# Self attention of a decoder layer: softmax sums as a ninth value column, division between two block transposes on DVE

## What is computed

```
# x: [8, 256, 128]; 16 heads of 8 features; all in float32
q, k, v = heads(x @ wq.T), heads(x @ wk.T), heads(x @ wv.T)     # [8, 16, 256, 8]
scores = einsum('bhtc,bhkc->bhtk', q, k) * 8 ** -0.5
scores = where(tril, scores, -inf)
attn = softmax(scores, axis=-1)                                 # exp(s - max) / sum of exp(s - max)
out = einsum('bhtk,bhkc->bhtc', attn, v)
x = layernorm(x + out.reshape(8, 256, 128) @ wo.T)
...                                                             # cross attention, then the experts
```

## Time and profile before

| what | us |
|---|---|
| median of 3 executions | 1145.12 (1144.67 to 1145.13) |
| the profiled execution, its own time | 1145.18 |
| its span, first to last instruction | 1143.1 |
| busy: PE, DVE, ACT, POOL | 1099.8, 879.7, 734.4, 539.8 |
| granted TensorE clock, mean | 0.998 of full speed |
| one batch of self attention (end to end) | 21.2 in the middle, 22.6 and 23.7 in the last full ones |
| self attention's last matmuls (line 692) | end at 193.9 |

### The profile page before, as it was taken

One profiled execution on the slowest core, in us unless ns is written; L12 is line 12 of the kernel. 1 busy time (PEld: TensorE's weight loads), 2 busy tenths in 40 slices (PEclk: granted clock), 3 DMA queues, 4 the chain that ended last, 5 costly groups with the idle time before them and its releaser, 6 DMA issues.

```text
span 1143.1 us, 27502 instructions
## 1 busy us (share of the span) xinstructions
PE 1099.8 (96%) x8781; PEld 945.9 (83%) x8781; DVE 879.7 (77%) x2778; ACT 734.4 (64%) x1754; POOL 539.8 (47%) x892
## 2 busy tenths in 40 slices
PE   6999988999999999999999999999999999999997
PEld 5888876788887887887888888888788887999997
DVE  7999998887787877777877878877878686655554
ACT  6999997766666766766765766666667565322221
POOL 4666774544564365446455445544644432400101
PEclk9999999999999999999999999999999999999999
DMA  2000011000000000000000000000000003000000
GB/s 93 7 7 11 7 44 37 3 11 1 1 1 11 2 1 11 1 1 11 2 1 1 11 2 1 2 1 2 1 2 1 2 1 97 2 10 6 7 10 11
DMA packets 14683, 12.38 MB, mean 11 GB/s; under 512 B 1360, under 2 KB 13648, under 8 KB 14416
## 3 DMA queue, kind: packets, MB, share of 16 engines
q1 hardware_dynamic: 14128, 10.43, 3.0%
q10 hardware_dynamic: 416, 0.20, 0.1%
HBM read 9.57 MB, written 1.05 MB: 9 GB/s over the span
## 4 chain that ended last, share of the span: by engine, by line
PE 65%; POOL 7%; issue 3%; ACT 1%; DVE 1%; POOLq 0%; DVEq 0%; ACTq 0%
PE ps L1163 12%; PE ps L1152 12%; PE ps L1146 11%; PE ps L1487 5%; POOL xk_parts L890 3%; PE ps L1478 3%; PE ps L1479 3%; PE ps L1480 3%; PE ps L1178 3%; PE ps L1136 2%; PE ps L1137 2%; PE ps L1138 2%; PE ps L1171 2%; PE ps L1118 2%; PE ps L1120 1%
## 5 line engine op out<-in xcount | busy, mean ns | idle before, releaser
L890 POOL TENSOR_TENSOR xk_parts<-k_raw,xk_parts 64x768 fp32r<-64x768 f32 x128 | 236.1, 1844 | 313.2 <-DVE xk_parts L1009 310.5
L1033 DVE CUSTOM_DVE_ANT_0 xmasked<-ps,bar 128x768 f32<-128x768 f32 x256 | 244.3, 954 | 4.3 <-issue 0.6
L946 ACT ACTIVATE xprobs<-xmasked,xlow 128x768 f32<-128x768 f32 x256 | 238.2, 930 | 1.3 <-DVE xlow L1033 1.0
L1146 PE MATMUL ps<-xk_parts,xq_parts 128*128 128x512 f32 (+1 forms) x1024 | 232.7, 349 | 2.7 <-ACT k_raw L926 1.3
L1152 PE MATMUL ps<-ident,xprobs 128*128 128x128 f32 x1536 | 215.2, 276 | 5.6 <-DVE xlow L1033 5.3
L1146 PEld LDWEIGHTS ps<-xk_parts,xq_parts 128*128 128x128 f32 x1024 | 173.7, 189 | 28.9 <-ACT k_raw L926 3.0
L1152 PEld LDWEIGHTS ps<-ident,xprobs 128*128 128x128 f32 x1536 | 168.8, 140 | 15.2 <-DVE xlow L1033 10.1
L1163 PE MATMUL ps<-xprobs_t,xvals 128*64 128x256 f32 x1536 | 179.9, 383 | 1.1 <-issue 1.1
L1163 PEld LDWEIGHTS ps<-xprobs_t,xvals 128*64 128x64 f32 x1536 | 104.8, 137 | 57.9 <-issue 11.9
L1038 DVE COPY xprobs_t<-ps 128x768 f32<-128x768 f32 x128 | 121.6, 950 | 2.0 <-PE ps L1152 2.0
L926 ACT ACTIVATE k_raw<-ps 128x768 f32<-128x768 f32 x64 | 52.0, 812 | 102.5 <-PE ps L1120 89.6
(11 more groups left out here) (220 smaller groups left out, 2526.9 us busy)
## 6 DMA issues: line engine op xcount, KB each, us to landing
ctx_in<-in_ctx SPq DMA_DIRECT2D x8, 256.0 KB, 3.2
w_rest<-in_L_ffn_w SPq DMA_DIRECT2D x2, 768.0 KB, 5.8
raw_kv<-in_L_xattn_Wkv SPq DMA_DIRECT2D x1, 1024.0 KB, 5.2
out<-state SPq DMA_DIRECT2D x8, 128.0 KB, 2.0
x_in<-in_x SPq DMA_DIRECT2D x7, 128.0 KB, 2.1
raw_q<-in_L_xattn_Wq SPq DMA_DIRECT2D x1, 512.0 KB, 6.0
wout<-in_L_xattn_Wout SPq DMA_DIRECT2D x1, 512.0 KB, 3.9
keep_all<-in_mask_BxS_bk SPq DMA_DIRECT2D x1, 512.0 KB, 5.2
```

The lines of the kernel that those rows point to most:

```text
L890: pool.tensor_tensor(k_parts[dst, i // 2 % 2, h, :], k_raw[src, :], k_parts[src, i // 2 % 2, h, :].bitcast(F32), ALU.subtract).then_inc(k_ ...
L946: nc.scalar.activation(probs[:, i % 4, :], masked[:, i % 4, :], ACT.Exp, scale=-1.0, bias=low[:, i % 4:i % 4 + 1], accum_out=sums[:, pair ...
L1033: dve.tensor_tensor_reduce(masked[:, i % 4, :], slot(slots.place("S", b, i), KEYS), bar[:, par, :], 1.0, 3e38, ALU.add, ALU.min, low[:, i ...
L1146: last = nc.tensor.matmul(slot(s, hi - lo, lo), q_parts[:, pair % 2, h, part, t * P:(t + 1) * P], k_parts[:, pair % 2, h, lo:hi], start=pa ...
```

## The change

The value blocks get a ninth column of ones, so that the PV matmuls give the sums of the exponentials beside the 8 features (row 32j+8 of the result for head j). The accumulator output of EXP is gone, and with it `sums`, `WIDE`, `R` and `rsum_t`. Per group DVE now does four steps: `TURN` transposes 32x32 blocks of the PV result, so that a token's features of a head stand side by side with their sum; `RECIP` takes the reciprocals of the sums; `DIVIDE` multiplies the 8 features by them; `NORM` transposes the blocks back into `heads_t`. PE's next PV into the same bank waits for TURN. Of the copies PT, ACT takes three of four heads and DVE the last of each group. The input is loaded into `state` directly, and OUT adds in place, so the loads don't wait for earlier batches. Setup gains two memsets on DVE. OUT moves to 24.5 in both tables, and a few cross attention steps on DVE (BAR, HI, TWICE) and the turn of its slots are shifted.

```diff
@@ DVE's steps of the cross attention that stand in the last units
-                               B: steps(emit, "Q", 1, 5, 1) + steps(emit, "BAR", 1, 7.6, 1) + steps(emit, "HI", 2, 5.8, 0.7)
-                               + steps(emit, "TWICE", 2, 6.2, 1.35)})
+                               B: steps(emit, "Q", 1, 5, 1) + steps(emit, "BAR", 1, 8.7, 1) + steps(emit, "HI", 2, 5.8, 1.4)
+                               + steps(emit, "TWICE", 2, 7.1, 1.5)})
...
-    x_in = sb(mem, "x_in", [P, 2, T, D])
...
-    sums = sb(mem, "sums", [P, 2, T, HG])
-    rsum = sb(mem, "rsum", [P, 2, T, HG])
-    rsum_wide = sb(mem, "rsum_wide", [P, 2, T, HG, 32])
-    rsum_t = sb(mem, "rsum_t", [P, 2, S])
+    turned = sb(mem, "turned", [P, 2, S // 32, 32])
+    rsum = sb(mem, "rsum", [P, 2, S // 32, 1])
+    divided = sb(mem, "divided", [P, 2, S // 32, 32])
...
+    def by_dve(h):
+
+        return h % HG == HG - 1
...
     pe_order = Order(B, SH, {
         "S": (SH, -0.5), "PT": (SH, 4.75), "K": (SG, -3.5), "Q": (SG, -4), "V": (1, 2),
-        "T": (1, -5), "R": (SG, 9.75), "PV": (SG, 9.5), "OUT": (1, 24),
+        "T": (1, -5), "PV": (SG, 9.5), "OUT": (1, 24.5),
...
     dve_order = Order(B, SH, {
-        "S": (SH, -0.5), "K": (SG, -3.5), "Q": (SG, -4.25), "PT": (SH // 2, 5.5),
-        "XLO": (1, -5.25), "RECIP": (SG, 5.75), "NORM": (SG, 10), "OUT": (1, 23.5),
+        "S": (SH, -0.5), "K": (SG, -3.5), "Q": (SG, -4.25), "PT": (SH, 4.5),
+        "XLO": (1, -5.25), "TURN": (SG, 10), "RECIP": (SG, 10.3), "DIVIDE": (SG, 10.6), "NORM": (SG, 11), "OUT": (1, 24.5),
...
-        "EXP": (SH, 3), "PT": (SH // 2, 6.75), "K": (SG, -1.75), "Q": (SG, -3), "R": (SG, 11.25),
+        "EXP": (SH, 3), "PT": (SH, 6.75), "K": (SG, -1.75), "Q": (SG, -3),
...
     pool_order = Order(B, SH, {
-        "Q_HEAD": (SH, 1.25), "WIDE": (SG, 10.75), "SPLIT": (3, 5.5, 5)})
+        "Q_HEAD": (SH, 1.25), "SPLIT": (3, 5.5, 5)})
...
@@ SP
-            wait(sp, added, b - 1)
             wait(sp, loaded_x, 16 * b)
-            sp.dma_start(x_in[:, par, :, :], x_rows[b]).then_inc(loaded_x, 16)
+            sp.dma_start(state[:, b * T:(b + 1) * T, :], x_rows[b]).then_inc(loaded_x, 16)
...
@@ ACT
-                if i % HG == 0:
-                    wait(act, rsum_ready, b * SG + g - 1)
...
                     nc.scalar.activation(probs[:, i % 4, lo:hi], masked[:, r, lo:hi], ACT.Exp,
-                                         scale=-1.0, bias=low[:, r, j:j + 1],
-                                         accum_out=sums[:, g % 2, j, i % HG:i % HG + 1]).then_inc(exp_done, 1)
+                                         scale=-1.0, bias=low[:, r, j:j + 1]).then_inc(exp_done, 1)
...
@@ DVE
-        dve.memset(vals[:, :, :, :, :], 0.0)
+        dve.memset(divided[:, :, :, :], 0.0)
+        link(dve.memset(vals[:, :, :, :, :], 0.0))
+        dve.memset(vals[:, :, :, :, SD:SD + 1], 1.0)
...
+            if kind == "TURN":
+                n = b * SG + i
+                dve.wait_ge(pv_done, n + 1)
+                wait(dve, divided_ready, n - 1)
+                dve.transpose(turned[:, i % 2, :, :].rearrange("p n c -> p (n c)"),
+                              ps[:, O_BANK + i % 2, 0:S]).then_inc(turned_ready, 1)
             if kind == "RECIP":
                 n = b * SG + i
-                dve.wait_ge(exp_done, T * HG * (n + 1))
-                wait(dve, wide_ready, n - 1)
-                dve.reciprocal(rsum[:, i % 2, :, :], sums[:, i % 2, :, :]).then_inc(rsum_ready, 1)
+                dve.wait_ge(turned_ready, n + 1)
+                dve.reciprocal(rsum[:, i % 2, :, :], turned[:, i % 2, :, SD:SD + 1]).then_inc(rsum_ready, 1)
+            if kind == "DIVIDE":
+                n = b * SG + i
+                dve.wait_ge(rsum_ready, n + 1)
+                wait(dve, heads_ready, n - 1)
+                dve.tensor_tensor(divided[:, i % 2, :, 0:SD], turned[:, i % 2, :, 0:SD],
+                                  rsum[:, i % 2, :, :].broadcast_to([P, S // 32, SD]), ALU.mult).then_inc(divided_ready, 1)
             if kind == "NORM":
                 n = b * SG + i
-                dve.wait_ge(rsum_t_ready, n + 1)
-                dve.wait_ge(pv_done, n + 1)
+                dve.wait_ge(divided_ready, n + 1)
...
-                dve.tensor_tensor(heads_t[:, i, :], ps[:, O_BANK + i % 2, 0:S], rsum_t[:, i % 2, :],
-                                  ALU.mult).then_inc(heads_ready, 1)
+                dve.transpose(heads_t[:, i, :], divided[:, i % 2, :, :].rearrange("p n c -> p (n c)")).then_inc(heads_ready, 1)
...
@@ PE, PV
-                pe.wait_ge(pt_act, (n + 1) * HG // 2)
-                pe.wait_ge(pt_dve, (n + 1) * HG // 2)
+                pe.wait_ge(pt_act, (n + 1) * (HG - 1))
+                pe.wait_ge(pt_dve, n + 1)
                 pe.wait_ge(v_ready, b + 1)
-                wait(pe, heads_ready, n - 1)
+                wait(pe, turned_ready, n - 1)
...
-    slots = Turns(pe_order, full, SLOTS, 2)
+    slots = Turns(pe_order, full, SLOTS, 1)
```

56 lines of the change are left out of this document (20 added, 36 removed).

## The result

The changed kernel is slower: 1148.53 us, median of 8 executions (1148.06 to 1148.94), against 1145.12 of the kernel before on the same chip; the ratio is 1.0029, with a 95% interval of 1.0020 to 1.0038. The prediction said 1142.3. The profiled execution has a span of 1146.5 us against 1143.1, so 3.4 us are to be found in the trace.

What follows compares the result with a forecast made beforehand. ACT was taken to bound the kernel, with DVE the bound afterwards. Against 1145.18 us, -4.0 for the batches, -0.4 for the late ones and +1.5 at the stage's end gave 1142.3 us; 8 in 10 range 1135 to 1152.

Steps and rivals of the forecast that it cites:

- What bounds the kernel before: Middle of the stage: ACT is the bound, busy 20.84 of 21.20 us a batch, with DVE busy 19.47.
- ACT after the change: ACT's work a batch falls from 20.7 to 18.2 us, with 0.70 a head instead of 0.88.
- DVE after the change: DVE's work a batch rises by 0.92 to 19.8 us, 1.14 added against 0.91 removed per group; DVE becomes the bound.
- The half rate case: Rival: DVE's 4-byte block transpose runs at half a copy's rate, giving a batch of 22.7 and 1158.7 us; chance 0.08.
- The meeting with POOL: DIVIDE on DVE is blocked while POOL masks heads, costing 0.4 us a batch; bounds 0 and 2.4.
- The rival in which every group meets a mask: DIVIDE meets a POOL head mask nearly each time, giving a batch of 21.7 to 21.8 and 1151.6 us; chance 0.18.
- Waits that stay: DVE's remaining stands at OUT, TURN and XLO cost 0.3 us a batch; bounds 0 and 1.0.
- Another limit close to 21 holds the pace: Rival: PE's matmuls or the PE, ACT and DVE loop around Q and K; 1144 to 1146.7 us; chance 0.26.
- The late batches: The two batches mixed with cross attention steps each take 0.2 us less, 0.4 together; bounds 1 us either way.
- The end of the stage: The last DIVIDE stalls beside POOL's 1.80 us instruction, delaying NORM and PE's OUT: 1.5 us more; bounds -0.5 and 2.5.
- The edits costed at nothing: The setup's two memsets fall in DVE's wait for weights, and loads without their wait change nothing: no cost or gain.

Runs made afterwards that it cites:

- The run with HI behind: The changed kernel with the cross attention's first HI step on DVE moved from ahead of the last TURN to behind the last NORM; 1146.26 us, ratio 1.0012.

## Why the prediction was wrong

**What bounds the kernel before: right.** ACT set the pace, and the kernel without accumulators fell by 1.0 us a batch. With them back in the changed kernel the pace rose by 0.3 only.

**ACT after the change: right.** 0.69 to 0.71 a head for the forecast 0.70, and by the starts over three batches 18.3 of work a batch for the forecast 18.2.

**DVE after the change: right in kind, 0.7 us a batch too small.** DVE did become the bound. Each term by its pitch: TURN 0.48 for 0.44; RECIP 0.16 in the mean for 0.11 (0.19 with a stand of 0.09 behind every fourth); DIVIDE 0.25 for 0.26; NORM 0.37 for 0.33. TURN and NORM lie within their bounds, which only shows how much four steps of a few hundredths come to: 0.16 and 0.16 a batch. RECIP had no bounds, since it seemed unchanged. But the old one, 8 columns of a buffer filled long before, overlapped the NORM behind it; the new one takes 0.15 to the next start, and once a batch 0.29 with a stand, 0.2 of work a batch more than forecast. Together the four steps are 0.5 above the forecast. The last 0.2 are in steps that the change left alone and the prediction took a little too short: S 0.58 for 0.57, OUT 0.42 for 0.33. The half rate case is out: a transpose out of PSUM costs nearly what a copy does (444 against 419 ns). The Trainium skill, page "Vector Engine (DVE) Microarchitecture Reference", section 3.8, says that the transpose sustains one element per cycle per lane, and the trace agrees in that it shows no half rate. Within SBUF a copy beats the transpose by 0.16 of pitch, though; the prediction had taken the row of a PSUM read for it, and so wasn't misled by this.

**The meeting with POOL: the size right, with luck.** Forecast 0.4 a batch, measured 0.39. The prediction took each group to meet a mask at random. In the trace it is the same group in each batch, the last one, that loses 0.39, and the other three lose nothing; kernels with other lists lose up to 0.6, or none. The rival in which every group meets a mask didn't come.

**Waits that stay: the step that failed, beside DVE's sum.** Forecast 0.3, with bounds of 0 and 1.0. The changed kernel has 0.33 ahead of XLO, 0.29 ahead of V, 0.13 behind OUT, 0.09 behind a RECIP and some hundredths in small pieces, about 0.9. The stand ahead of OUT, the only one that the prediction sized, did go. The error is one of method: the prediction took the whole of 21.2 minus 18.8 for room that ACT's slowness made. 0.7 of this 2.4 was never idle, since the earlier trace rows has DVE busy 19.47, and its starts from OUT to OUT sum to 19.5 too. The pitches were read where the queue is full; ahead of a stand an instruction costs its whole length, a PT copy 0.55 and not 0.47. Of the 1.7 that is left, 1.0 stayed in the kernel before without accumulators, when ACT was no longer in the way. These aren't the same stands as in the changed kernel, since 0.7 of them are ahead of OUT; the run shows that about as much stays as the changed kernel has, and not that the same stands do. With 0.9 in the place of 0.3 the pace would have been forecast at 21.1 and the time at about 1145.5, no change. With 0.7 more work of DVE besides it is 21.8, which is what was measured. It took both errors to turn the sign of the pace.

Together: 20.5 was forecast, 21.76 measured; 0.7 of the difference is work of DVE and 0.6 are waits. Over the 5.4 batch lengths up to the OUT at 128.8 the forecast was -4.0, and +3.25 came (+0.87, +1.66 and +0.72).

**The rivals.** None of them came as it was written. "Another limit close to 21 holds the pace" has the nearest time, 1146.7 at its end, and there is such a limit: the kernel with all copies on ACT stops at 21.4. But in the changed kernel DVE's own sum and stands came first.

**The late batches: right.** Forecast -0.4 together, measured -0.60.

**The end of the stage: the size right by luck, by half another mechanism.** Forecast +1.5, measured +1.43 from OUT to OUT. DIVIDE did take 1.26 beside POOL's 1.79, as worked out. But against the OUT before it the last OUT on PE came no later for that (177.74 to 194.71, 16.97 us, where it was 175.09 to 192.14, 17.05). The 193.9 in the table ahead of the prediction is where the last of these matmuls starts; they end at 194.2. What made OUT on DVE late was PE's clock, 3.56 us for matmuls that took 2.02. The run with HI behind shows the two parts: OUT on PE 1.4 earlier, and 1.5 from the clock. With the meeting and without the fall of the clock, as in the profile of V on ACT, the stretch is 19.03, no longer than the 19.14 before. The forecast had the stall and did not have the clock.

**The edits costed at nothing,** the two memsets of the setup and the loads without their wait, show nothing: the first wide score step of DVE starts at 13.27, where it was 13.44. They weren't tried alone. The first batch's 0.87 wasn't taken apart by a run of its own, but DVE is near full there too: from 20.00 to 44.58 it is busy 23.86 of 24.58, and without DIVIDE the first OUT comes at 42.50.

## What to carry to other kernels

When one engine is relieved, the idle time of the next one is not its room, and a sum of pitches below its busy time overstates even that (18.8 here, against 19.47). Look at each stand of it by releaser, and ask whether that releaser is the relieved engine's own queue or a chain that stays; a run that relieves the first engine and adds nothing to the second measures how much stays in one go. Put new work on the engine that really has time: here POOL waited 29 us in three batches, and the same change with the division there is 0.6% faster than before instead of 0.3% slower. And where a change lengthens a stand of PE, read the granted clock behind it.
